# Causal attention stage: both score products of a step issued together on four row groups, its weights turned by ordinary products with the identity, and the sign of the row maximum moved to ScalarE

## The chip, the cores and the metric

One core of a Trainium2 chip. The metric is the device time of one execution in microseconds, the median of several runs: 5253.66 us before (5250.62 to 5260.75, three runs).

## The reference

Input x has 8 sequences of 512 tokens with 256 features. Four residual blocks follow each other, each on a layer norm of x: attention a (8 heads of 64), a feed-forward block f of two layers (each with windowed attention and a gated MLP), the causal attention b, and f again. All is float32. The change touches only b, which has 16 heads of 16 features:

```python
dot = jnp.einsum('bhid,bhjd->bhij', q, k)
q_norm_sq = jnp.sum(q * q, axis=-1, keepdims=True)
k_norm_sq = jnp.sum(k * k, axis=-1, keepdims=True)
vals = q_norm_sq + k_norm_sq.transpose(0, 1, 3, 2)
scores = dot * dot / (vals - 2.0 * dot + EPSILON) * SCORE_SCALE
mask = jnp.triu(jnp.ones((Lq, Lq), dtype=scores.dtype), k=1) * -1000000000.0
attn = jax.nn.softmax(scores + mask[None, None, :, :], axis=-1)
out = jnp.einsum('bhij,bhjd->bhid', attn, v)
```

So a score needs two numbers of each pair of tokens: a denominator (the squared distance plus epsilon) and the dot product for the numerator.

## The kernel before, in words

The work is a list of 48 units: 6 stages (`PLAN`: a, f, f, b, f, f) times 8 sequences. All weights of a stage are loaded once, and the activations of all sequences stay in SBUF (`resid`). Stage b is units 24 to 31.

A unit of stage b has 32 steps (`BSTEPS`). A step is two heads and one tile of 128 queries; query tile t = i % 4 sees 128 (t+1) keys, so a step's width w is 128, 256, 384 or 512 columns for each head. A step consists of parts, named in the code by `kind`:

- `bk`, `bq` (TensorE): turn 128 rows of k and q so that the features lie on partitions. A head takes 32 partitions (`BROW`), of which 16 are features and two more carry the squared norms and ones. Before the change one filling holds four heads (one per 32 rows), is done by four transposes of 128x128, and serves 8 steps; there are 4 fillings of each per unit. `bk_c`, `bq_c` (ScalarE) copy them to `k_rows`, `q_rows` (in the tile `hid`).
- `bden` (TensorE): the denominator, 18 rows deep, for the two heads; `bdot`: the dot product, 16 rows deep, for the two heads. Each is two products, on two different 32-row groups of the array; `bden` and `bdot` of a head lie on the same row group. Each takes one of the three PSUM tiles of two banks, `wide0` to `wide2`.
- `bclip` (VectorE, L1197, L1199) bounds the denominator and puts it into `b_den` (tile `w_up`); `bnum` (ScalarE, L1016) squares the numerator into `prob`.
- `bguess` (ScalarE, L1027 logarithm, L1029 exponential) makes a first reciprocal, `bclose` (GpSimd, L1414) and the first half of `bmul` (VectorE, L1207) refine it; `bmul` (VectorE, L1214, twice) multiplies it into the weights and takes each row's extreme; a last VectorE instruction of two columns (L1218) turns its sign (semaphore `neg`).
- `exp` (ScalarE, L1056, one for each head) waits for `neg`; `mask` (GpSimd, L1420) zeroes what lies above the diagonal.
- `turn_a`, `turn_b` (TensorE, L697): 2 (t+1) transposes of 128x128 into one wide tile; `pt_a` (ScalarE, L1064) and `pt_b` (VectorE, L1253) copy them out; `mix` (TensorE, L694, tile `o_ps`) multiplies them with v, two heads on two 32-column groups.
- After 8 steps `out`, `sel`, `olog`, `out_b` divide by the row sums. `proj` and `res` end the unit. The next unit's layer norm, `xt` and `bqkv` (128x512 and 128x256 products, `w_in`) run among the steps.

L694 and L697 are the lines of the helpers `mm` (matmul) and `tr` (transpose), so PE rows are told apart by their tiles. A float32 `mm` shows as two MATMUL and two LDWEIGHTS records, a `tr` as one of each.

Nothing in the engines' programs reorders work: `ordered()` writes each engine's order in advance, by a greedy pass over the parts with the costs in `cost()` and `B_COST`, the due times and the lists of what a part follows; each engine then executes its list in order, with semaphore waits in front of each part. The same pass places PSUM holders: three wide tiles and the narrow `turn_ps` (for `bk`, `bq`, `sel`). New costs thus change the order of all of stage b. Rings: `prob` has 4 buffers in stage b, `b_den`/`b_inv` 3, `pt` 2, `q_rows`/`k_rows` 2 each.

Of the kernel before, what the change touches and what calls it, by code (L numbers as in the profile page):

```python
# [8 lines left out]
ALU = mybir.AluOpType  # L9
# [62 lines left out]
for _e, _kinds in {  # L72
# [5 lines left out]
    for _k in _kinds.split():  # L78
# [3 lines left out]
B_COST = {"bclip": (0.15, 0.27), "bnum": (0.1, 0.27), "bguess": (0.25, 0.54), "bclose": (0.2, 0.6), "bmul": (0.6, 0.55),  # L82
          "exp": (0.25, 0.26), "turn_a": (0.05, 0.14), "turn_b": (0.05, 0.14), "pt_a": (0.12, 0.135),
          "pt_b": (0.12, 0.135), "mix": (0.1, 0.25), "mask": (0.8, 0.0)}


def cost(kind, u, i):
# [6 lines left out]
    if kind in ("bden", "bdot"):  # L94
        return 0.25 + 0.23 * (i % 4 + 1)
# [31 lines left out]
def parts_of(u):  # L127
# [94 lines left out]
    for k in range(steps):  # L222
# [5 lines left out]
        if st == "b":  # L228
            g = k // 8
            if k % 8 == 0:  # L230
                for kind in ("bk", "bq"):
                    put(kind, g, at - 4 / steps, final("brow", 3))
                    free = (u, 8 * (g - 1) - 1) if g >= 2 else (u - 1, 8 * (g + 3) - 1)
                    put(kind + "_c", g, at - 4 / steps, final(kind, g), ("bden", *free), ("bdot", *free),
                        ("down", u - 1, 3))
            put("bden", k, at, final("bk_c", g), final("bq_c", g))
            put("bdot", k, at, final("bk_c", g), final("bq_c", g))
            three = (u, k - 3) if k >= 3 else (u - 1, k + steps - 3)
            put("bclip", k, at, final("bden", k), ("bmul", *three), ("up_h", u - 1, 2))
# [98 lines left out]
def ordered():  # L338
# [14 lines left out]
    def ready_at(part):  # L353

        if part not in ready:
# [8 lines left out]
            for r in READERS.get(kind, ()):  # L364
                for f in parts.get((r, u, i), (0, ()))[1]:
                    if f in parts and f[0] != kind and f[0] not in READERS[kind]:
# [106 lines left out]
def build(nc, d):  # L473
    stack = ExitStack()
    with stack:
# [188 lines left out]
        def rows_free(gate, u, g):  # L664

            if g >= 2:
                gate.wait_ge(S["bden"], nth("bden", u, 8 * (g - 1) - 1))
                gate.wait_ge(S["bdot"], nth("bdot", u, 8 * (g - 1) - 1))
            elif u > 3 * SEQS:
                gate.wait_ge(S["bden"], nth("bden", u - 1, 8 * (g + 3) - 1))  # L670
                gate.wait_ge(S["bdot"], nth("bdot", u - 1, 8 * (g + 3) - 1))
# [18 lines left out]
        def tensor_program(eng):  # L690
# [9 lines left out]
            for part in ORDER["PE"]:  # L700
# [80 lines left out]
                elif kind in ("bk", "bq"):  # L781
                    pe.wait_ge(S["brow"], nth("brow", u, TILES - 1))
                    src = (k_t if kind == "bk" else q_t)[s]
                    for t in range(TILES):
                        last = tr(turn_ps[:, t * P:(t + 1) * P], src[:, i, t * P:(t + 1) * P])
# [26 lines left out]
                elif kind in ("bden", "bdot"):  # L812
                    g, t = i // 8, i % 4
                    pe.wait_ge(S["bk_c"], nth("bk_c", u, g))
                    pe.wait_ge(S["bq_c"], nth("bq_c", u, g))
                    for k in range(2):
                        r = 32 * (2 * (i // 4 % 2) + k)
                        rows = slice(r, r + BHD + (2 if kind == "bden" else 0))
# [798 lines left out]
```

## Time and profile before

| | |
|---|---|
| median of three runs | 5253.66 us |
| the profiled execution, its own time | 5240.19 us |
| its span (first to last instruction) | 5238.2 us |
| mean granted TensorE clock over the span | 0.888 |
| busy: PE, DVE, ACT, POOL | 92%, 66%, 49%, 45% |
| first and last L1218 of stage b (256 of them) | 2285.2 and 3724.0 us |

PE is TensorE's matmul record, DVE is VectorE, ACT ScalarE, POOL GpSimd. Full clock, 1.00, is 2.4 GHz, and 0.50 is 1.2 GHz. Durations of matmuls include the way through the array, so several in a row take less than their sum.

### The profile page before, as it was taken

Reading aid. Unit: us, or ns where it says so; the run is one execution under the profiler, and the core shown is the slowest. Engines: PE = TensorE matmul, PEld = TensorE weight load, DVE = VectorE, ACT = ScalarE, POOL = GpSimd, SP = SyncE. Lnnn points to the kernel's source line nnn. Section 1 sums busy time; section 2 is a strip of 40 time slices with the busy share of each in tenths; the row PEclk is TensorE's granted clock in tenths of the full one; section 3 lists DMA queues with packets and bytes.
Section 4 is the critical chain, followed back from the end, with each engine's and each line's share of the span. In section 5 each row is a group of like instructions: output and inputs, shape, how many; then the busy total and the mean of one; then the engine's idle time right before and its main releaser. Section 6 shows DMA issues by size and latency. Waiting matters only on the chain.

```text
span 5238.2 us, 66473 instructions
## 1 busy us (share of the span) xinstructions
PE 4802.2 (92%) x23008; PEld 2828.5 (54%) x23008; DVE 3440.7 (66%) x8032; ACT 2581.4 (49%) x5577; POOL 2332.9 (45%) x2331
## 2 busy tenths in 40 slices
PE   7878888999999999999999999999799999999997
PEld 4444445655555555555555555545455555555564
DVE  4554566666666666468888888878766666666653
ACT  4443444444444444356666666666544444444442
POOL 1111244544544454344555555555544544545441
PEclk9999999999999999975666666757899999999998
DMA  2000000000000000000000000000000000100000
GB/s 63 9 5 9 21 5 11 3 5 3 21 7 26 11 7 13 18 8 1 5 5 5 1 9 5 5 13 5 26 5 3 3 5 19 30 11 17 15 15 21
DMA packets 50974, 60.82 MB, mean 12 GB/s; under 512 B 11848, under 2 KB 43216, under 8 KB 50640
## 3 DMA queue, kind: packets, MB, share of 16 engines
q1 hardware_dynamic: 50640, 56.58, 3.5%
q8 instruction: 184, 3.01, 0.2%
q14 instruction: 150, 1.23, 0.1%
HBM read 35.61 MB, written 12.58 MB: 9 GB/s over the span
## 4 chain that ended last, share of the span: by engine, by line
PE 74%; DVE 15%; issue 4%; ACT 3%; POOL 3%; DMA 1%; SPq 1%; POOLq 0%; DVEq 0%; ACTq 0%
PE wide L694 51%; PE o_ps L694 10%; PE wide L697 6%; PE turn_ps L697 5%; DVE prob L1227 2%; DVE x_n L1101 1%; DVE st L1234 1%; POOL rn L1397 1%; DMA shifted<-resid 1%; DVE pt L1253 1%; DVE prob L1214 1%; SPq L1455 1%; PE turn_ps L694 1%; DVE w_down L1214 1%; ACT pt L1064 1%
## 5 line engine op out<-in xcount | busy, mean ns | idle before, releaser
L1427 POOL TENSOR_SCALAR prob<-prob,st 128x256 f32<-128x256 f32 (+1 forms) x1024 | 521.4, 529 | 972.5 <-DVE st L1240 972.2
L694 PE MATMUL wide<-w_in,x_t 128*128 128x512 f32 (+1 forms) x1792 | 850.5, 621 | 4.6 <-DVE w_up L1199 1.8
L694 PE MATMUL o_ps<-pt,v 128*64 128x256 f32 (+2 forms) x5632 | 646.9, 376 | 119.7 <-DVE pt L1253 63.9
L694 PE MATMUL wide<-x_t,w_up 128*128 128x512 f32 (+1 forms) x1536 | 698.9, 601 | 16.8 <-DVE k_t L1161 11.4
L1064 ACT ACTIVATE pt<-turn_ps 128x512 f32<-128x512 f32 x384 | 229.3, 597 | 850.4 <-PE turn_ps L697 850.4
L694 PEld LDWEIGHTS o_ps<-pt,v 128*64 128x64 f32 (+1 forms) x5632 | 391.2, 142 | 397.1 <-issue 186.1
L694 PE MATMUL wide<-hid 16*128 16x128 f32 (+7 forms) x2048 | 560.9, 662 | 41.7 <-DVE w_up L1199 27.7
L697 PE MATMUL turn_ps<-ident,prob 128*128 128x128 f32 x2816 | 466.1, 285 | 126.6 <-ACT pt L1064 122.6
L1035 ACT ACTIVATE prob<-prob,st 128x256 f32<-128x256 f32 (+1 forms) x1024 | 478.9, 472 | 189.8 <-DVE st L1227 189.7
L694 PEld LDWEIGHTS wide<-w_in,x_t 128*128 128x128 f32 x1792 | 350.2, 205 | 387.2 <-issue 379.2
L697 PEld LDWEIGHTS turn_ps<-ident,prob 128*128 128x128 f32 x2816 | 315.2, 142 | 417.9 <-issue 234.4
L694 PEld LDWEIGHTS wide<-x_t,w_up 128*128 128x128 f32 (+1 forms) x1536 | 260.7, 179 | 368.9 <-issue 347.8
L1253 DVE COPY pt<-turn_ps 128x384 f32<-128x384 f32 (+1 forms) x384 | 227.8, 593 | 299.5 <-PE turn_ps L697 299.5
L1389 POOL TENSOR_TENSOR sines<-raw,rot 128x512 f32<-128x512 f32 x256 | 386.8, 1530 | 54.8 <-ACT raw L959 54.8
L1397 POOL TENSOR_TENSOR rn<-ss,minus_half 128x16 f32<-128x16 f32 x128 | 381.1, 2977 | 51.5 <-DVE ss L1147 51.0
L1138 DVE TENSOR_TENSOR turned<-raw,rot 128x512 f32<-128x512 f32 x256 | 237.7, 969 | 229.4 <-ACT raw L959 228.5
L694 PE MATMUL wide<-k_t,q_t 64*128 64x256 f32 (+2 forms) x2560 | 364.4, 421 | 3.6 <-DVE resid L1269 2.0
L1227 DVE CUSTOM_DVE_ANT_0 prob<-wide,local_mask 128x256 f32<-128x256 f32 (+1 forms) x1024 | 332.5, 385 | 49.6 <-PE wide L694 49.6
L1430 POOL TENSOR_SCALAR prob<-prob,st 128x512 f32<-128x512 f32 x128 | 125.3, 981 | 517.7 <-DVE st L1243 517.6
L694 PEld LDWEIGHTS wide<-hid 16*128 16x128 f32 (+1 forms) x2048 | 226.2, 262 | 232.4 <-issue 157.9
L694 PE MATMUL wide<-w_out,o_t 128*128 128x256 f32 x1536 | 345.7, 384 | 5.6 <-DVE o_t L1262 2.6
L694 PE MATMUL wide<-w_down,hid 128*128 128x256 f32 x1536 | 349.3, 381 | 1.6 <-DVE hid L1325 1.6
(137 smaller groups left out, 8187.6 us busy)
## 6 DMA issues: line engine op xcount, KB each, us to landing
kept<-resid SPq DMA_DIRECT2D x16, 512.0 KB, 2.6
x_n<-kept SPq DMA_DIRECT2D x16, 512.0 KB, 3.3
shifted<-resid SPq DMA_DIRECT2D x32, 224.0 KB
w_in<-in_f_wqkv SPq DMA_DIRECT2D x4, 1536.0 KB, 6.3
w_up<-in_f_w SPq DMA_DIRECT2D x4, 1364.0 KB, 6.1
resid<-in_x SPq DMA_DIRECT2D x8, 512.0 KB, 8.2
out<-resid SPq DMA_DIRECT2D x8, 512.0 KB, 2.9
w_down<-in_f_w SPq DMA_DIRECT2D x4, 640.0 KB
```

The lines of the kernel that those rows point to most:

```text
L694: return eng.matmul(out, lhsT, rhs, start=start, stop=stop, skip_group_check=True)
L697: return eng.transpose(out, in_, ident[:, :])
L1035: last = eng.activation(pr[:, local_span(t)], pr[:, local_span(t)], ACT.Exp, bias=sm[:, t:t + 1], scale=-1.0, accum_out=sm[:, 4 + t:5 + t])
L1064: eng.activation(pt[:, 0:w], ps[:, 0:w], ACT.Copy).then_inc(S["pt_a"], 1)
L1138: last = eng.tensor_tensor(heads(out[:, side]), heads(r[:, side]), rot[:, 2 * z, i, :].unsqueeze(1).to_broadcast([P, HEADS, HD]), ALU.mult)
L1214: last = eng.tensor_tensor_reduce(pr[:, side], pr[:, side], inv[:, side], -1.0, -LOW, ALU.mult, ALU.max, sm[:, 8 + k:9 + k])
L1227: eng.tensor_tensor_reduce(pr[:, local_span(t)], ps[:, local_span(t)], local_mask[:, P if t == 0 else 0:256], -1.0, LOW, ALU.add, ALU.min, ...
L1253: eng.tensor_copy(pt[:, 512:512 + w], ps[:, 0:w]).then_inc(S["pt_b"], 1)
L1389: last = eng.tensor_tensor(halves(sines[(o - 1) % 2][:, side]), halves(r[:, side])[:, :, ::-1, :], rot[:, 2 * z + 1, i, :].rearrange("p (u ...
L1397: eng.tensor_tensor(rn[(o - 1) % 2][:, 0:16], ss[(o - 1) % 2][:, 0, :], minus_half[:, 0:16], ALU.pow).then_inc(S["rn"], 1)
L1427: last = eng.tensor_scalar(pr[:, local_span(t)], pr[:, local_span(t)], sm[:, 8 + t:9 + t], 1.0, ALU.mult, ALU.mult)
L1430: last = eng.tensor_scalar(pr[:, 0:512], pr[:, 0:512], sm[:, 4:5], 1.0, ALU.mult, ALU.mult)
```

## The change

- `bk`, `bq`: 8 fillings of each per unit, one for every 4 steps. A filling now holds two heads, each twice, in the order head 0, head 0, head 1, head 1 on the four 32-row groups. It is made by 16 ordinary products of 128 rows by 32 columns with the identity as the moving side (128 columns), each writing 32 partitions of `turn_ps`.
- `bdot` issues all four products: denominator of both heads on row groups 0 and 2, dot product of both on row groups 1 and 3. `bden` stays in the order as a part without instructions, which takes its wide tile.
- `turn_a`, `turn_b`: the transposes become ordinary products with the identity.
- The two-column change of sign goes from VectorE to ScalarE, ahead of `exp`.
- The planner's costs and lists follow.

```diff
-B_COST = {"bclip": (0.15, 0.27), "bnum": (0.1, 0.27), "bguess": (0.25, 0.54), "bclose": (0.2, 0.6), "bmul": (0.6, 0.55),
-          "exp": (0.25, 0.26), "turn_a": (0.05, 0.14), "turn_b": (0.05, 0.14), "pt_a": (0.12, 0.135),
-          "pt_b": (0.12, 0.135), "mix": (0.1, 0.25), "mask": (0.8, 0.0)}
+B_COST = {"bclip": (0.15, 0.27), "bnum": (0.1, 0.22), "bguess": (0.2, 0.47), "bclose": (0.2, 0.6), "bmul": (0.5, 0.63),
+          "exp": (0.45, 0.26), "turn_a": (0.05, 0.16), "turn_b": (0.05, 0.16), "pt_a": (0.06, 0.12),
+          "pt_b": (0.12, 0.135), "mix": (0.1, 0.28), "mask": (0.85, 0.0)}
...
-        return 0.25 + 0.23 * (i % 4 + 1)
+        return 0.1 + 0.28 * (i % 4 + 1) if kind == "bdot" else 0.0
...
-            put("bden", k, at, final("bk_c", g), final("bq_c", g))
-            put("bdot", k, at, final("bk_c", g), final("bq_c", g))
+            last = ("bdot", u, k - 1) if k else ("bdot", u - 1, steps - 1)
+            put("bden", k, at, final("bk_c", g), final("bq_c", g), last, *turned, ("down", u - 1, 3))
+            put("bdot", k, at, final("bk_c", g), final("bq_c", g), final("bden", k))
...
                     for t in range(TILES):
-                        last = tr(turn_ps[:, t * P:(t + 1) * P], src[:, i, t * P:(t + 1) * P])
+                        for r in range(4):
+                            at = t * P + BROW * (2 * (i % 2) + r // 2)
+                            last = mm(turn_ps[r * BROW:(r + 1) * BROW, t * P:(t + 1) * P], src[:, i // 2, at:at + BROW],
+                                      ident[:, :], True, True)
...
-                elif kind in ("bden", "bdot"):
-                    g, t = i // 8, i % 4
+                elif kind == "bden":
+                    continue
+                elif kind == "bdot":
+                    g, t = i // 4, i % 4
                     pe.wait_ge(S["bk_c"], nth("bk_c", u, g))
                     pe.wait_ge(S["bq_c"], nth("bq_c", u, g))
-                    for k in range(2):
-                        r = 32 * (2 * (i // 4 % 2) + k)
-                        rows = slice(r, r + BHD + (2 if kind == "bden" else 0))
-                        last = mm(ps[:, 512 * k:512 * k + P * (t + 1)], q_rows[g % 2][rows, t * P:(t + 1) * P],
-                                  k_rows[g % 2][rows, 0:P * (t + 1)], True, True)
-                    last.then_inc(S[kind], 1)
+                    for what in ("bden", "bdot"):
+                        for k in range(2):
+                            r = 2 * BROW * k + (BROW if what == "bdot" else 0)
+                            rows = slice(r, r + BHD + (2 if what == "bden" else 0))
+                            last = mm(wide[PLACE[what, u, i]][:, 512 * k:512 * k + P * (t + 1)],
+                                      q_rows[g % 2][rows, t * P:(t + 1) * P], k_rows[g % 2][rows, 0:P * (t + 1)], True, True)
+                        last.then_inc(S[what], 1)
...
-                        last = tr(ps[:, to + kb * P:to + (kb + 1) * P],
-                                  prob[SLOTS[u, i]["prob"]][:, at + kb * P:at + (kb + 1) * P])
+                        last = mm(ps[:, to + kb * P:to + (kb + 1) * P], prob[SLOTS[u, i]["prob"]][:, at + kb * P:at + (kb + 1) * P],
+                                  ident[:, :], True, True)
...
                     exp_tables()
+                    act.wait_ge(S["bmul"], nth("bmul", u, i))
+                    eng.activation(sm[:, 0:2], sm[:, 8:10], ACT.Copy, scale=-1.0).then_inc(S["neg"], 1)
                     act.wait_ge(S["neg"], nth("bmul", u, i))
...
                     last.then_inc(S["bmul"], 1)
-                    dve.wait_ge(S["bmul"], o)
-                    eng.tensor_scalar(sm[:, 0:2], sm[:, 8:10], -1.0, None, ALU.mult).then_inc(S["neg"], 1)
```

## Rows read from the trace of the kernel before

**Rows 1.** The page's slices: busy tenths in 40 slices of the span, and granted clock.
```profile
PE   7878888999999999999999999999799999999997
PEclk9999999999999999975666666757899999999998
```

**Rows 2.** Windows of stages a, f, b: length, busy us of each engine (instructions), clock.
```profile
30.00:700.00 670.00, 555.79 (x2820) 309.36 (x2820) 341.35 (x586) 292.85 (x659) 146.27 (x137) 0.97 0.02 9
852.00:2296.00 1444.00, 1359.08 (x6338) 826.34 (x6337) 903.21 (x2347) 615.87 (x1469) 690.64 (x747) 0.99 0.04 11
...
2300.00:3700.00 1400.00, 1313.21 (x6533) 739.67 (x6532) 1147.76 (x2434) 944.92 (x1715) 720.01 (x617) 0.66 0.01 5
```

**Rows 3.** Chain of waits, shares by line, 2869 to 2917 us.
```profile
by line: PE wide L694 49.2%; PE wide L697 24.5%; PE o_ps L694 17.3%; PE turn_ps L697 4.4%; PE turn_ps L694 4.2%; DVE w_up L1199 0.9%; issue 0.1%
```

**Rows 4.** Windows: a cold stretch, then one at full clock (columns of Rows 2).
```profile
2869.00:2917.00 48.00, 47.74 (x193) 26.27 (x194) 38.98 (x90) 32.88 (x59) 27.85 (x23) 0.50 0.00 1
...
2916.00:2941.00 25.00, 22.87 (x148) 12.74 (x148) 22.85 (x49) 17.55 (x33) 12.76 (x10) 0.91 0.00 1
```

**Rows 5.** Groups in stage b: count, busy us, mean ns, idle before.
```profile
L694 PE MATMUL wide<-hid 18*128 18x384 f32 (+1 forms) x1984 | 545.5, 664 | 39.3 <-DVE w_up L1199 27.7 <-DVE pt L1253 4.6 <-ACT sq L962 3.3
...
L1218 DVE TENSOR_SCALAR st<-st 128x2 f32<-128x2 f32 x248 | 134.6, 543 | 8.6
```

**Rows 6.** Windows of L697, all transposes: stages a and b (PE, PEld, clock).
```profile
30.00:700.00 670.00, 155.78 (x972) 105.17 (x972) 0.97 0.02 9
...
2300.00:3700.00 1400.00, 343.78 (x1559) 249.12 (x1558) 0.66 0.01 5
```

**Rows 7.** Windows around one rise and fall of the clock.
```profile
2654.20:2661.00 6.80, 6.63 (x15) 3.21 (x16) 5.21 (x12) 2.73 (x7) 3.34 (x4) 0.50 0.00 0
2661.00:2688.00 27.00, 26.73 (x176) 17.20 (x176) 22.59 (x50) 19.07 (x35) 14.84 (x18) 1.00 0.05 21
2691.90:2730.00 38.10, 37.68 (x171) 21.16 (x169) 29.70 (x68) 25.68 (x47) 20.61 (x18) 0.50 0.00 1
```

**Rows 8.** Timeline of PE at full clock: start, duration of the run of records.
```profile
2917.44 1.04 PE L697 MATMUL wide<-ident,w_down 128*128 128x128 f32 x8
2918.41 0.85 PE L694 MATMUL o_ps<-pt,v 128*32 128x128 f32 x12
2919.18 1.99 PE L694 MATMUL wide<-hid 18*128 18x512 f32 x8
2921.47 1.07 PE L694 MATMUL o_ps<-pt,v 128*32 128x128 f32 x16
...
2937.05 1.13 PE L694 MATMUL wide<-hid 18*128 18x512 f32 x4
```

**Rows 9.** Timeline of PE at half clock.
```profile
2952.46 1.50 PE L694 MATMUL o_ps<-pt,v 128*32 128x128 f32 x12
2953.88 2.08 PE L694 MATMUL wide<-hid 18*128 18x512 f32 x4
2955.89 1.11 PE L697 MATMUL turn_ps<-ident,q_t 128*128 128x128 f32 x4
2956.80 1.91 PE L697 MATMUL wide<-ident,w_down 128*128 128x128 f32 x8
```

**Rows 10.** Groups of ACT in stage b by shape: smallest copy, smallest exponential, a filling's copy.
```profile
L1064 ACT ACTIVATE pt<-wide 128x128 f32<-128x128 f32 x62 | 16.7, 269 | 0.0
L1056 ACT ACTIVATE prob<-prob,st 128x128 f32<-128x128 f32 x124 | 42.4, 391 | 2.4 <-DVE st L1218 2.4
L1008 ACT ACTIVATE hid<-turn_ps 128x512 f32<-128x512 f32 x30 | 17.6, 587 | 0.0
```

**Rows 11.** Line L1218: durations ns min/median/max, first and last start.
```profile
L1218 DVE TENSOR_SCALAR st<-st x256: 168/169/2321, 2285.2 to 3724.0; 128x2 f32<-128x2 f32 x128
```

**Rows 12.** Timeline: GpSimd and VectorE side by side.
```profile
2916.42 1.81 POOL L1414 TENSOR_TENSOR w_up<-w_up,x_t 128x768 f32<-128x768 f32 x1 [0.65 <-ACT x_t L1029]
2916.45 1.81 DVE L1218 TENSOR_SCALAR st<-st 128x2 f32<-128x2 f32 x1
```

More of the change, by code:

```diff
@@ L228, in parts_of @@
         if st == "b":
-            g = k // 8
-            if k % 8 == 0:
+            g = k // 4
+            if k % 4 == 0:
                 for kind in ("bk", "bq"):
                     put(kind, g, at - 4 / steps, final("brow", 3))
-                    free = (u, 8 * (g - 1) - 1) if g >= 2 else (u - 1, 8 * (g + 3) - 1)
-                    put(kind + "_c", g, at - 4 / steps, final(kind, g), ("bden", *free), ("bdot", *free),
-                        ("down", u - 1, 3))
-            put("bden", k, at, final("bk_c", g), final("bq_c", g))
-            put("bdot", k, at, final("bk_c", g), final("bq_c", g))
+                    free = (u, 4 * (g - 1) - 1) if g >= 2 else (u - 1, 4 * (g + 7) - 1)
+                    put(kind + "_c", g, at - 4 / steps, final(kind, g), ("bdot", *free), ("down", u - 1, 3))
+            last = ("bdot", u, k - 1) if k else ("bdot", u - 1, steps - 1)
+            put("bden", k, at, final("bk_c", g), final("bq_c", g), last, *turned, ("down", u - 1, 3))
+            put("bdot", k, at, final("bk_c", g), final("bq_c", g), final("bden", k))
             three = (u, k - 3) if k >= 3 else (u - 1, k + steps - 3)
-            put("bclip", k, at, final("bden", k), ("bmul", *three), ("up_h", u - 1, 2))
+            put("bclip", k, at, final("bdot", k), ("bmul", *three), ("up_h", u - 1, 2))
             put("bnum", k, at, final("bdot", k), *turned, ("down", u - 1, 3))
@@ L365, in ready_at @@
                 for f in parts.get((r, u, i), (0, ()))[1]:
-                    if f in parts and f[0] != kind and f[0] not in READERS[kind]:
+                    if f in parts and f[0] != kind and f[0] not in READERS[kind] and f != ("bdot", u, i):
                         if f not in end:
@@ L666, in rows_free @@
             if g >= 2:
-                gate.wait_ge(S["bden"], nth("bden", u, 8 * (g - 1) - 1))
-                gate.wait_ge(S["bdot"], nth("bdot", u, 8 * (g - 1) - 1))
+                gate.wait_ge(S["bdot"], nth("bdot", u, 4 * (g - 1) - 1))
             elif u > 3 * SEQS:
-                gate.wait_ge(S["bden"], nth("bden", u - 1, 8 * (g + 3) - 1))
-                gate.wait_ge(S["bdot"], nth("bdot", u - 1, 8 * (g + 3) - 1))
+                gate.wait_ge(S["bdot"], nth("bdot", u - 1, 4 * (g + 7) - 1))
             else:
```

## The prediction

> **What bounds the kernel now.** I read the page's slices first [rows 1]: TensorE (PE) is above 90% busy nearly everywhere, and its granted clock is near 1 except in twelve slices in the middle, which are stage b. The windows put numbers on it [rows 2]: stage f has PE at 94% and clock 0.99; stage b has PE at 94% too (1313 of 1400 us) but clock 0.66, with DVE at 82%, ACT at 67% and POOL at 51%. The 256 steps of b span about 1440 us [rows 11]. The chain of waits over a cold stretch is 99% PE [rows 3], and there PE is busy 47.7 of 48.0 us while DVE has 39.0 [rows 4]. At nearly full clock the picture turns: in 2916 to 2941 DVE is busy 22.85 of 25 us, PE 22.87 and with idle gaps. So b is bound by PE at half clock, and DVE stands right behind it.
>
> Why is the clock low? PE is no less busy than in f. What differs is the kind of work: 545 us of b's PE time are score products 16 or 18 rows deep on two 32-row groups [rows 5], 344 us are transposes [rows 6]; together two thirds. The clock rose after a stretch of few, long records that fill the array (15 matmul records in 6.8 us) and fell back among steps (171 in 38 us), with PE 97 to 99% busy on both sides [rows 7]. Transposes alone don't do it: stage a has 156 us of them in 670 us and a clock of 0.97, but its other products are 64 to 128 rows deep. Thus shallow products and transposes together leave the clock low, by these rows.
>
> **The change part by part**, PE first, at full clock (2.4 GHz); at half clock (1.2 GHz) it takes about double.
>
> Scores. A score product of 512 columns and its partner take 1.13 us, denominator and numerator together 1.99 us [rows 8]. Per 128 columns a single float32 product costs about 0.22 us: mix goes from 0.85 us (12 records, three rounds of two side by side) to 1.07 us (16 records, four rounds). With four products side by side a step of tile t saves 0.22 (t+1) us, on average 0.22 x 2.5 = 0.545, x256 = 140 us. That four run together is not in the trace; two do. Bound from the other side: two at a time, saving nothing. I take four, since they use disjoint row groups as the two do now.
>
> Turns. A transpose costs (1.04 - 0.17)/8 = 0.109 us, an ordinary product two records of that, 0.218. There are 2 (t+1) per step, 5 on average: 5 x 0.109 = 0.545, x256 = 140 us more. Scores and turns cancel, at either clock.
>
> Fillings. There are 64 of bk and bq now, 1.11 us each at half clock [rows 9], 0.60 at full (4 x 0.109 + 0.17). After, 128, each 16 products on four column groups: four rounds of two records, eight slots of 0.109 plus 0.2 = 1.07 us (1.9 at half clock). That adds 128 x 1.07 - 64 x 0.60 = 98 us at full clock, 172 at half. If only two column groups work together, as mix shows, it is 128 x 0.87 = 111 us more; if products with the half-sized weight side cost less, at most the 98 goes.
>
> So at an unchanged clock PE has about 100 to 170 us more to do. Everything hangs on the clock. Work of 1313 us at a mean of 0.66 is 867 us at full clock, some 890 with the fixed 0.2 us of each run of products; plus 98 is about 990, at a clock of 0.97 (stage a's) 1015 us per 1400 us of today's stage. And the clock should come: of a step's PE time after the change the turns (1.3 us of about 3.7) and the fillings (0.5) fill the array with ordinary products, the scores hold four row groups in place of two, and mix and bqkv stay. Full-array work per stage rises by 140 x 2 + 128 x 0.87 = 390 us within some 1200. That is denser than stage a, which holds 0.97 with PE only 83% busy.
>
> On this point the Trainium skill has a sentence in each direction. "TensorE: Matmul & The Clock Gate", Part 4, says a transpose-mode product doesn't count as busy for the clock; by it the turns alone would lift the clock, and the trace agrees as far as b's cold stretches are rich in them. "Perfetto Trace Analysis", section Transposes, says to use transposes, not standard matmuls, for a transpose; by it the change of the turns is a loss. No row here shows a float32 product with the identity that is not a transpose; by the rows of mix it costs what is written above under Turns, and the second rival carries it.
>
> VectorE. L1218 goes: 134.6 us per 1400 [rows 5]. Its median is 169 ns, its mean 543 [rows 11]: the rest is waiting beside a GpSimd instruction, seen at 2916.45, where both last 1.81 us [rows 12]. Part of that wait may reappear at L1214, next to which POOL runs more densely: I add 30 (bounds 0 and 90). DVE: 1148 - 135 + 30 = 1043.
>
> ScalarE. It gets 256 copies of two columns. The trace has no such shape; the smallest copy of 128 columns takes 0.269 us, the smallest exponential 0.391 [rows 10]. Taking 0.25 near the former: 248 x 0.25 = 62 (40 to 97); queued behind it are this step's two exponentials, which waited for L1218 anyway. Plus 64 more copies of fillings at 0.587, 37 us. ACT: 945 + 62 + 36 = 1043. GpSimd keeps 720.
>
> So three engines have 1015 to 1043 us each in place of one with 1313. What share can the busiest reach? DVE reached 0.91 in the stretch at high clock [rows 4], where PE had slack; with three equals and orders fixed in advance I take 0.89: 1043/0.89 = 1172, times 1440/1400 = 1206 us. Saved: 1440 - 1206 = 234. The profiled execution took 5240.2 (2 outside the span), so 5006; the median of the three stands 13.5 above it, so about **5020**. At 0.94 (PE in f) it is 1141 and 4955; at 0.83 (PE in a) 1292 and 5106.
>
> What is late next: DVE, mostly at L1214 and L1207, with ACT on its heels; the edge of PSUM too, since both scores now want two of three wide tiles at once.
>
> **Rivals.**
>
> 1. Clock rises, but the queues block each other. bdot starts only when two wide tiles are free, the turns hold the third, and the next step's scores wait for L1197/L1199 on a DVE that is full. Holding times per step are about 2.0 (denominator), 1.8, 2.0 and 1.0 for the unit's other products, 6.8 us over three tiles or 2.3 us a step against 4.7 available: for it speaks only that PE's queue is in order; against it the slack. Price: half a microsecond a step on the 1206, 128 us: 5020 + 128 = 5150.
>
> 2. The other side: the clock stays. It decides if the granted clock of b remains below about 0.8. PE then carries scores and turns that cancel, plus fillings, 98 to 172 us, about 150, at 94 to 99% busy; nothing else matters. 5254 + 150 = 5400. For it: PE was 97% busy in the cold and that didn't help, so density must really change; against it, stage a.
>
> 3. Scores run two at a time. PE gets 140 us more, 1155 per 1400, and binds again: at 0.94, 1229, times 1.03 = 1264 us, 5078. For it: no four at once in the trace.
>
> **How the numbers follow.** Forecast 0.62; rival 1, 0.16; rival 2, 0.10; rival 3, 0.12. The likeliest time is 5020. Its own range, from the shares 0.94 and 0.83 and the bounds of ACT and DVE, is 4940 to 5110; to leave out only about 2 in 10 I stretch it over the third rival and the first: 4930 to 5185. A measurement of this kernel can tell about 0.2% (10 us) from no change. Faster: 0.87, the forecast and rivals 1 and 3, less a little for fillings that cost more than I think; slower 0.10, rival 2; same 0.03.
>
> **What the profile after would show.** Right: b's granted clock above 0.93; score records of 16 and 18 rows starting together, and a run of 512 columns for both lasting 1.1 to 1.3 us; eight turns as 16 records in about 1.9 us; fillings of 32 records in about 1.1 us; L1218 gone, a two-column ACT copy of 0.2 to 0.3 us; DVE near 88% busy in b; its chain mixed of DVE, PE and ACT; stages a and f unchanged to 10 us. Wrong: clock in b below 0.8 and a chain all of PE (rival 2); at full clock, PE idle on L1199 or L1016 with DVE under 80% (rival 1); score runs of 1.9 us at full clock (rival 3).

## The result, and the profile after

The changed kernel takes 5186.4 us (median of four runs, 5166.7 to 5202.4) against 5252.1 us: a ratio of 0.9872 with a 95% interval of 0.9835 to 0.9910. It is faster by 66 us, where 5020 us was forecast with a range of 4930 to 5185. The time lies 1.4 us outside the range, and the gain is little more than a quarter of the forecast 232 us. The profiled execution is the fastest of the four, 5166.7 us.

The page's slices after, beside [rows 1]: tenths of busy time, and the granted clock.
```profile
PE   7878888999999999998888888878899999999997
...
PEclk9999999999999999998888898889899999999998
```
In the middle PE fell from 9 to 8 tenths (7 in one slice) while the clock rose from 5 to 8 tenths to 8 and 9. The other slices are unchanged or nearly so. The window of stage b after, columns as in [rows 2]: length, then busy us (instructions) of PE, PEld, DVE, ACT and POOL, clock.
```profile
2290.00:3668.00 1378.00, 1154.70 (x11777) 817.28 (x11768) 1091.02 (x2273) 1059.22 (x2092) 759.72 (x645) 0.87 0.02 6
```
The steps of b span 1372 us (first to last start of the instruction shown below), where they spanned 1439 [rows 11]: 67 of the 74 us by which the profiled execution is shorter (span 5164.3 us for 5238.2). No engine is at 90%: PE has 84%, DVE 79%, ACT 77%, POOL 55%. The chain of waits of stage b, by line, first before (2300 to 3700 us), then after (2300 to 3600 us):
```profile
by line: PE wide L694 39.0%; PE wide L697 16.3%; PE o_ps L694 13.1%; issue 4.7%; DVE prob L1214 3.4%; PE turn_ps L694 3.3%; DVE w_down L1214 2.9%; PE turn_ps L697 2.7%; DVE x_t L1207 2.2%; DVE x_n L1207 2.1%; DVE hid L1207 2.0%; DVE w_up L1
```
```profile
by line: PE wide L692 33.6%; issue 9.5%; PE o_ps L692 7.2%; PE turn_ps L692 6.1%; DVE prob L1220 5.2%; POOL w_up L1418 4.6%; DVE w_down L1220 4.1%; DVE hid L1213 2.5%; DVE x_t L1213 2.3%; ACT prob L1062 2.2%; DVE x_n L1213 1.7%; DVE shifted
```
The lines of PE had 74% of the chain before and have 47% after; PE is still its largest part, with the other engines now sharing the rest. "Issue" is time in which an engine waited for nothing that the profile shows. `mm` is now L692 and `tr` L695, so a turn by a product stands under L692.

The single operations, from PE's timeline (start, us; beside [rows 8]):
```profile
2862.07 2.05 PE L692 MATMUL wide<-ident,w_down 128*128 128x128 f32 x16 [0.36 <-DVE raw L1183]
...
2867.08 1.07 PE L692 MATMUL o_ps<-pt,v 128*32 128x128 f32 x16
2868.08 1.14 PE L692 MATMUL wide<-hid 18*128 18x512 f32 x8
2869.15 1.08 PE L692 MATMUL turn_ps<-ident,k_t 128*32 128x128 f32 x32
```
Denominators and dot products of 512 columns together take 1.14 us, where they took 1.99; a filling of 16 products takes 1.08; eight turns take 2.05, where the transposes took 1.04 and I had reckoned with 1.9. The same timeline, a little earlier, shows what the mean hides:
```profile
2852.59 1.65 PE L692 MATMUL turn_ps<-ident,q_t 128*32 128x128 f32 x32 [2.95 <-DVE o_t L1266]
...
2875.08 0.71 PE L692 MATMUL wide<-hid 18*128 18x256 f32 x8 [1.96 <-ACT prob L1020]
```
PE stood for 2.95 us before the filling, the clock fell to half at 2852.9 while the filling ran, and it took 1.65 us in place of 1.08. The pause of 1.96 us is followed by the next fall, at 2876.8.
```profile
2852.00:2860.00 8.00, 6.67 (x60) 4.96 (x61) 4.86 (x11) 3.15 (x7) 1.03 (x1) 0.57 0.00 0
```
The line is the window of those 8 us, columns as before: PE's clock is 0.57. Over the stage PE idles 223 us (1378 - 1155). The trace's clock falls to half 56 times within the steps of b, for 341 us in all and never for more than 10.3 us at a time; before, it fell 32 times, for 980 us in all and up to 181 us at a time.

ScalarE's new instruction, as the view of its line shows it: durations in ns (min/median/max), first and last start.
```profile
L1058 ACT ACTIVATE st<-st x256: 186/196/224, 2296.6 to 3668.4; 128x2 f32<-128x2 f32 x128
```

### The profile page after: what moved, and what is told of

Same layout as the page of the kernel before. It is cut to its first block, busy times and chain, and to the rows that moved or that the text cites. A ratio compares the mean times of both kernels' runs of the same rounds, so it can differ in the third digit from the quotient of the medians.

```text
span 5164.3 us, 76918 instructions
## 1 busy us (share of the span) xinstructions
PE 4604.0 (89%) x28128; PEld 2885.9 (56%) x28128; DVE 3328.0 (64%) x7776; ACT 2660.6 (52%) x5897; POOL 2332.1 (45%) x2331
## 4 chain that ended last, share of the span: by engine, by line
PE 67%; DVE 16%; ACT 6%; issue 5%; POOL 4%; DMA 1%; SPq 1%; DVEq 0%; POOLq 0%; ACTq 0%
PE wide L692 50%; PE o_ps L692 9%; PE turn_ps L695 5%; PE wide L695 2%; PE turn_ps L692 2%; DVE prob L1231 2%; DVE prob L1220 1%; DVE x_n L1107 1%; POOL w_up L1418 1%; DMA shifted<-resid 1%; DVE st L1238 1%; DVE w_down L1220 1%; DVE pt L1257 1%; ACT pt L1070 1%; SPq L1459 1%
## 5 line engine op out<-in xcount | busy, mean ns | idle before, releaser
L692 PE MATMUL wide<-w_in,x_t 128*128 128x512 f32 (+1 forms) x1792 | 828.9, 608 | 2.3 <-ACT x_t L956 1.3
L692 PE MATMUL o_ps<-pt,v 128*64 128x256 f32 (+2 forms) x5632 | 598.8, 353 | 186.8 <-DVE pt L1257 82.5
L692 PE MATMUL wide<-x_t,w_up 128*128 128x512 f32 (+1 forms) x1536 | 697.8, 601 | 15.7 <-DVE k_t L1167 11.4
L692 PEld LDWEIGHTS o_ps<-pt,v 128*64 128x64 f32 (+1 forms) x5632 | 369.2, 133 | 430.5 <-issue 168.3
L695 PE MATMUL turn_ps<-ident,prob 128*128 128x128 f32 x2816 | 467.6, 286 | 125.8 <-ACT pt L1070 121.3
L695 PEld LDWEIGHTS turn_ps<-ident,prob 128*128 128x128 f32 x2816 | 316.3, 142 | 420.6 <-issue 237.8
L692 PEld LDWEIGHTS wide<-w_in,x_t 128*128 128x128 f32 x1792 | 339.8, 200 | 361.9 <-issue 357.3
L692 PEld LDWEIGHTS wide<-x_t,w_up 128*128 128x128 f32 (+1 forms) x1536 | 260.5, 179 | 367.6 <-issue 347.7
L692 PE MATMUL wide<-k_t,q_t 64*128 64x256 f32 (+2 forms) x2560 | 362.2, 419 | 2.3 <-DVE k_t L1167 2.2
L692 PE MATMUL wide<-w_down,hid 128*128 128x256 f32 x1536 | 349.1, 381 | 1.6 <-DVE hid L1329 1.6
L692 PE MATMUL wide<-w_out,o_t 128*128 128x256 f32 x1536 | 339.9, 379 | 2.0 <-ACT o_t L1080 1.9
L692 PEld LDWEIGHTS wide<-w_out,o_t 128*128 128x128 f32 x1536 | 291.0, 190 | 56.3 <-issue 18.4
L692 PEld LDWEIGHTS wide<-w_down,hid 128*128 128x128 f32 x1536 | 284.8, 190 | 39.6 <-DVE hid L1329 2.5
```

The source lines that it names most:

```text
L692: return eng.matmul(out, lhsT, rhs, start=start, stop=stop, skip_group_check=True)
L695: return eng.transpose(out, in_, ident[:, :])
```

## The experiments

In every edit below, orders of all engines stay as in the kernel named, unless it says that they change. Ratios are against the kernel before, run beside it on the same chip, with 95% intervals.

**First round: each part undone or done alone.** The theory then was that the products with the identity lift the clock and that this is the gain.

e1, the changed kernel with transposes for the turns:
```diff
-                        last = mm(ps[...], prob[...][...], ident[:, :], True, True)
+                        last = tr(ps[...], prob[...][...])
```


> The changed kernel with its turns of stage b as transposes again; every engine's order as in the changed kernel. Theory (the products with the identity are what lifted the clock): the granted clock of stage b falls from 0.87 to about 0.70 and the time rises to 5230 to 5300 us although TensorE has 140 us less to do at full clock. Rival (four row groups and the column-tiled fillings lifted the clock): the clock stays at 0.85 or more and the time falls to 5100 to 5150 us.

Measured: 5132.6 us, ratio 0.9769 (0.9751 to 0.9786), 54 us faster than the change, and the theory fell. The window of its stage b, columns as above:
```profile
2292.00:3654.00 1362.00, 1097.64 (x10538) 687.18 (x10528) 1076.24 (x2276) 1061.44 (x2096) 756.13 (x645) 0.79 0.02 6
```
The clock did fall, from 0.87 to 0.79, but not to where it had been, and PE is busy 57 us less all the same. The products lift the clock and cost more than they lift. The 140 us of added work at full clock came out as 57 us of busy time. Not all of that is time of the stage: PE's idle is 41 us longer in e1 (264 for 223), and from first to last instruction of the sign the steps span 1353 us for 1372. The 54 us are between medians; how the profiled executions divide their 31 us is told behind the third round.

e4, the reverse: the kernel before with only the turns as products (the edit of e1 the other way round).

> The kernel before with only its turns of stage b as ordinary products with the identity; orders, layout and costs of before kept. Theory (the products lift the clock and that is the whole gain): the clock of stage b rises from 0.66 to 0.85 or more, and although TensorE gets 140 us more at full clock the time falls to 5130 to 5210 us. Rival (the other parts lifted the clock; by itself the product is only dearer than a transpose): the clock stays below 0.75 and the time rises by 100 to 280 us to 5350 to 5530.

Measured: 5253.5 us, ratio 1.0012 (0.9998 to 1.0027): no change. The window of its stage b:
```profile
2289.00:3742.00 1453.00, 1314.33 (x7975) 871.88 (x7975) 1185.18 (x2512) 981.32 (x1767) 747.72 (x635) 0.81 0.01 5
```
The same window of the kernel before:
```profile
2281.00:3724.00 1443.00, 1348.31 (x6714) 759.21 (x6716) 1184.23 (x2514) 975.14 (x1767) 741.15 (x635) 0.66 0.01 5
```
The clock rose from 0.66 to 0.81 by this edit alone, PE is busy 34 us less, and nothing came of it. So clock and time are different things here. Neither the theory (a gain) nor its rival (a loss) was right: gain of clock and cost of work cancel in the kernel before, and e1 shows a loss in the changed one.

e2, both dot products on the row groups of the denominators:
```diff
-                            r = 2 * BROW * k + (BROW if what == "bdot" else 0)
+                            r = 2 * BROW * k
```


> The changed kernel with both dot products on the row groups of the denominators, so that only two of the four score products can run together; orders kept. Theory (TensorE's length still counts in stage b): a run for 512 columns lasts 2.0 us in place of 1.14, 140 us more work at full clock, the time rises by 60 to 140 us to 5250 to 5330. Rival (stalls of the in-order queue set the time and absorb it): less than 30 us more.

Measured: 5246.5 us, ratio 0.9987 (0.9977 to 0.9996), so four at once are worth 60 us in the changed kernel, of 140 us of work at full clock, at the lower edge of the 60 to 140 expected.

e3, the sign back on VectorE:
```diff
-                    act.wait_ge(S["bmul"], nth("bmul", u, i))
-                    eng.activation(sm[:, 0:2], sm[:, 8:10], ACT.Copy, scale=-1.0).then_inc(S["neg"], 1)
...
+                    dve.wait_ge(S["bmul"], o)
+                    eng.tensor_scalar(sm[:, 0:2], sm[:, 8:10], -1.0, None, ALU.mult).then_inc(S["neg"], 1)
```


> The changed kernel with the change of sign back on VectorE; orders kept. Theory (VectorE's port waits count): the instruction takes about 0.5 us again on the mean, the time rises by 30 to 80 us to 5215 to 5265. Rival (neither engine is the bound, each at under 0.8 of the stage): within 15 us of 5186.

Measured: 5256.0 us, ratio 1.0007 (0.9994 to 1.0020): 70 us more, all of the change's gain. The instruction is the old one again, with a median of 169 ns and a longest of 2374, in the view of its line:
```profile
L1222 DVE TENSOR_SCALAR st<-st x256: 168/169/2374, 2304.5 to 3762.1; 128x2 f32<-128x2 f32 x128
```
ScalarE stood 180 us until this instruction, ahead of the exponentials; in the changed kernel it stands 103 us ahead of its own copy. The window of stage b:
```profile
2300.00:3763.00 1463.00, 1179.26 (x11743) 838.93 (x11744) 1203.32 (x2530) 1023.44 (x1837) 759.91 (x645) 0.86 0.02 5
```
The stage is 85 us longer than the change's, PE is busy only 25 us of them and idle the other 60: here the sign costs through waits, not through PE's clock.

**Second round: does the smallest edit do it alone, and is the plan to blame?**

e5, the kernel before with only the sign on ScalarE (the edit of e3 reversed).

> The kernel before with only the change of sign moved to ScalarE; orders, layout, costs and transposes of before kept. Theory (several engines share the path, and this one edit shortens VectorE by 0.47 us a step wherever it is put): the time falls by 40 to 80 us to 5170 to 5210. Rival (before, TensorE at half clock is the only bound, 93% busy, so VectorE's relief is hidden and pays only once TensorE is relieved): within 20 us of 5252.

Measured: 5206.8 us, ratio 0.9903 (0.9873 to 0.9934), 51 us less by the ratio, although PE still was the busiest engine by far, as the window of its stage b shows:
```profile
2294.00:3691.00 1397.00, 1283.93 (x6712) 728.36 (x6710) 1086.54 (x2257) 1017.93 (x2022) 737.30 (x635) 0.70 0.01 5
```
PE is 92% busy here, at a clock of 0.70. That relief on an engine at 82% shortens a stage in which PE has 94% speaks against the reading that PE's work alone is the bound. It doesn't show through what it came: the clock rose from 0.66, and PE's busy time fell by 64 us at the same work (1348 x 0.66 = 890, 1284 x 0.70 = 899), which is more than the stage's 46.

e6, e1 with each filling by four transposes (it leaves out the doubling of the heads, so the scores mix heads):
```diff
-                        for r in range(4):
-                            at = t * P + BROW * (2 * (i % 2) + r // 2)
-                            last = mm(turn_ps[r * BROW:(r + 1) * BROW, t * P:(t + 1) * P], src[:, i // 2, at:at + BROW],
-                                      ident[:, :], True, True)
+                        last = tr(turn_ps[:, t * P:(t + 1) * P], src[:, i // 2, t * P:(t + 1) * P])
```


> As e1 (changed kernel, turns as transposes), with each filling of k and q made by four transposes of 128x128 in place of 16 products. This leaves out the doubling of the heads, so denominators and dot products of a step are of different heads; amounts and orders are the same. It prices the fillings. Theory (they cost 0.5 us each at full clock, 128 of them, and lift the clock little): the time falls by 30 to 60 us against e1's 5133, clock 0.74 to 0.79. Rival (the fillings' products are what lifts e1's clock to 0.79 from 0.66): the clock falls to 0.70 or less and the time rises above 5150.

Measured: 5133.9 us, ratio 0.9760 (0.9728 to 0.9792), the same as e1, where 30 to 60 us less was expected. The steps of b tell it otherwise: they span 1332 us, 20 us less than e1's 1353, with PE's work at full clock 65 us less (1078 x 0.74 = 798 for 1092 x 0.79 = 863). The rest of the program took 14 us longer in the profiled execution than in e1's, and hides it. One execution of each tells no more than that the fillings may cost some 20 us. The edit gives back only what 16 products cost more than four transposes, 60 of the 98 us that I had priced (128 x (1.07 - 0.60)); that there are twice as many fillings stays in.

e10, e1 with measured costs in the planner (orders change):
```diff
-B_COST = {"bclip": (0.15, 0.27), "bnum": (0.1, 0.22), "bguess": (0.2, 0.47), "bclose": (0.2, 0.6), "bmul": (0.5, 0.63),
-          "exp": (0.45, 0.26), "turn_a": (0.05, 0.16), "turn_b": (0.05, 0.16), "pt_a": (0.06, 0.12),
+B_COST = {"bclip": (0.2, 0.29), "bnum": (0.1, 0.22), "bguess": (0.2, 0.47), "bclose": (0.2, 0.6), "bmul": (0.6, 0.8),
+          "exp": (0.5, 0.3), "turn_a": (0.1, 0.13), "turn_b": (0.05, 0.13), "pt_a": (0.13, 0.12),
...
-            "bk": 0.6, "bq": 0.6, "proj": 1.9, "xt2": 1.2, "up_g": 3.6, "up_h": 3.6, "down": 2.8,
+            "bk": 1.05, "bq": 1.05, "proj": 1.9, "xt2": 1.2, "up_g": 3.6, "up_h": 3.6, "down": 2.8,
```


> As e1, with the planner's costs of stage b set to what the trace measured (fillings 1.05 in place of 0.6, VectorE's multiplication 0.6 + 0.8 per 128 columns in place of 0.5 + 0.63, exponentials, bounding and copies a little more, transposes 0.13 per block), so all orders of stage b change. Theory (the idle of 16 to 20% on TensorE comes from orders planned with costs that are too small): TensorE idles less, the time falls by 20 to 60 us against e1 to 5075 to 5115. Rival (the waits come from the dependencies and the three PSUM tiles, not from the costs): within 20 us of 5133.

e11, e1 with `sel` in a wide tile (orders change):
```diff
-NARROW = ("bk", "bq", "turn_a", "turn_b", "sel")
+NARROW = ("bk", "bq", "turn_a", "turn_b")
...
-                    mm(turn_ps[:, :], sum_rows[:, :], o_raw, True, True).then_inc(S["sel"], 1)
+                    mm(ps[:, 0:512], sum_rows[:, :], o_raw, True, True).then_inc(S["sel"], 1)
...
-                    eng.activation(b_weight, turn_ps[:, :], ACT.Ln).then_inc(S["olog"], 1)
+                    eng.activation(b_weight, wide[PLACE["sel", u, i]][:, 0:512], ACT.Ln).then_inc(S["olog"], 1)
...
```


> As e1, with the product of the row sums (sel) in one of the three wide PSUM tiles in place of turn_ps, so that the fillings no longer wait for the division of the group before. Theory (the waits of the fillings for o_t, some 37 us of TensorE's idle in the changed kernel, end the path): 15 to 40 us less than e1's 5133. Rival (the wide tiles are scarcer than the narrow one): 10 to 60 us more.

Measured: e10 5141.9 us (0.9779, 0.9753 to 0.9806) and e11 5151.5 us (0.9793, 0.9759 to 0.9827). Better costs don't help, and neither does freeing the narrow tile; both theories missed. In the profiled executions the steps of b span 1346 and 1351 us, where e1's span 1353.

**Third round: what holds all engines at 80%?**

e14, e1 with GpSimd's product in `bclose` cut to 16 columns (most of the refinement is left out):
```diff
-                    eng.tensor_tensor(den, den, inv, ALU.mult).then_inc(S["bclose"], 1)
+                    eng.tensor_tensor(den[:, 0:16], den[:, 0:16], inv[:, 0:16], ALU.mult).then_inc(S["bclose"], 1)
```


> As e1, with GpSimd's product in bclose cut to 16 columns of a step's 256 to 1024, which leaves most of the refinement of the reciprocal out. GpSimd loses about 370 of its 756 us in stage b, and VectorE the waits beside it. Theory (the engines walk in lockstep, the path goes through all of them, GpSimd's latency too): the time falls by 80 to 160 us against e1's 5133 although GpSimd is only 56% busy. Rival (GpSimd is off the path): less than 40 us.

Measured: 5008.8 us, ratio 0.9534 (0.9514 to 0.9554), 124 us below e1. The window of its stage b:
```profile
2290.00:3502.00 1212.00, 1025.82 (x10537) 645.33 (x10526) 971.59 (x2275) 1052.36 (x2093) 412.18 (x645) 0.84 0.02 6
```
With this product out of the way the stage is 1212 us long, and the busiest engine, now ScalarE, reaches 87%. That this is nearly the 1206 us that I had forecast is in part luck: DVE has 972 us here and PE 1026, less than the changed kernel's 1091 and 1155. DVE lost 105 us of busy time (55 of them in the multiplications into the weights, L1220, and 25 in L1213) though its work is unchanged, so that much was waiting inside its instructions beside GpSimd; PE lost 72, and times the clock its work is the same (1098 x 0.79 = 867, 1026 x 0.84 = 862). The chain of waits of the changed kernel had given the product only 4.6% (POOL w_up L1418), 60 us of 1300: cutting it was worth twice that.

e15, e1 with four buffers between `bclip` and `bmul`, in all units but the last (orders change; the waits for a free buffer change with it and aren't shown):
```diff
-        b_inv = [..., b_hid[:, 2048:3072]]
+        b_den.append(sines[0][:, :])
+        b_inv = [..., b_hid[:, 2048:3072], sines[1][:, :]]
```


> As e1, with four buffers for the denominators and reciprocals in place of three (the fourth in the tiles of the sines, which stage b does not use; the last unit keeps three); the orders change with it. Theory (the ring between bclip and bmul, 8 us long and three steps deep, keeps the engines at 0.79): the time falls by 20 to 60 us. Rival (PSUM and PE's order set the pace): within 20 us of 5133.

e18, e1 with `HOP = 0.35` for 0.2 (orders change):

> As e1, with the planner's time for a hop between engines at 0.35 in place of 0.2, which changes the orders of all stages. Theory (orders matter by chance only, a per cent either way): within 40 us of 5133. Rival (the plan is too tight for the real hops): 20 to 60 us less.

e20, e1 with denominators and dot products as two parts again (orders change, and so do the parts' costs and the waits for them):
```diff
-            put("bden", k, at, final("bk_c", g), final("bq_c", g), last, *turned, ("down", u - 1, 3))
-            put("bdot", k, at, final("bk_c", g), final("bq_c", g), final("bden", k))
+            put("bden", k, at, final("bk_c", g), final("bq_c", g))
+            put("bdot", k, at, final("bk_c", g), final("bq_c", g))
...
-                    for what in ("bden", "bdot"):
+                    for what in (kind,):
...
```


> As e1, with denominators and dot products of a step as two parts again, each with its own tile and wait, on the new row groups, so that the denominator can start when one wide tile is free; orders change. Theory (the demand for two of three wide tiles at once stalls TensorE, my first rival): the time falls by 20 to 60 us, TensorE's idle ahead of the scores shrinks. Rival (what four at once gains is lost when the two parts come apart): 20 to 80 us more.

Measured: e15 5150.9 us (0.9807, 0.9793 to 0.9822), e18 5179.4 (0.9864, 0.9842 to 0.9887), e20 5181.9 (0.9871, 0.9852 to 0.9890). A fourth buffer doesn't help. e18 is 47 us worse, more than the 40 expected, and e20 costs 49 us against e1.

Here the whole times mislead. The steps of b, from the first to the last instruction of the sign, and all that lies before and behind them, in the profiled execution of each kernel (us; e21 and e22 are of the fourth round):

| kernel | span | steps of b | before and behind |
|---|---|---|---|
| before | 5238.2 | 1438.8 | 3799.4 |
| the change | 5164.3 | 1371.8 | 3792.5 |
| e1 | 5133.4 | 1352.7 | 3780.7 |
| e6 | 5126.9 | 1332.4 | 3794.5 |
| e10 | 5142.5 | 1345.5 | 3797.0 |
| e11 | 5150.8 | 1350.7 | 3800.1 |
| e14 | 4991.8 | 1204.1 | 3787.7 |
| e15 | 5153.4 | 1351.3 | 3802.1 |
| e18 | 5171.8 | 1342.7 | 3829.1 |
| e20 | 5172.0 | 1366.3 | 3805.7 |
| e21 | 5067.6 | 1284.5 | 3783.1 |
| e22 | 5181.5 | 1389.3 | 3792.2 |

What lies behind the steps, with the same work, first in the change and then in e1:
```profile
3668.40:5164.30 1495.90, 1389.88 (x6481) 848.19 (x6480) 895.63 (x2351) 625.82 (x1516) 672.49 (x732) 0.97 0.05 15
```
```profile
3652.70:5133.40 1480.70, 1373.80 (x6466) 839.47 (x6464) 896.11 (x2351) 625.88 (x1516) 673.83 (x732) 0.98 0.05 15
```
So of the 31 us between these two executions 19 are the steps' and 15 lie behind them (ahead of them 3 us go the other way). Behind them PE was busy 16 us less at a clock of 0.98 for 0.97. Of all the runs only e1 and e21 have 0.98 there. Why they do is open. One execution of each is profiled, and those of the changed kernel differ by 36 us among themselves, so the steps are known to some 20 us.

With that, e10, e11, e15 and e18 are not worse than e1 in the stage that they were made for: 1343 to 1351 us for 1353. e18's 47 us lie outside the steps, since `HOP` changes the orders of all stages. Four other plans of b thus move its steps by 10 us at most, where 166 are to be explained (1372 for the forecast 1206). That is evidence against a large effect of the costs, the narrow tile, the ring or the hop, and no evidence on smaller ones.

e20 doesn't settle what it was made for. PE's timeline in it:
```profile
2864.55 0.70 PE L694 MATMUL wide<-hid 18*128 18x256 f32 x4
2869.30 1.22 PE L694 MATMUL wide<-hid 16*128 16x256 f32 x4 [4.05 <-DVE w_up L1205]
```
Denominators and dot products come apart by over 4 us, and within the steps PE is busy 1191 us for e1's 1092. The edit takes away the demand for two tiles at once and the four at once together. That the steps lose only 14 us by it leaves room for a gain from the first. The waits of PE in the changed kernel, 2300 to 3600 us (us in total, times, longest), say more:
```profile
PE o_ps L692 <- ACT pt L1070: 53.9, 33, 3.0
...
PE wide L692 <- ACT prob L1020: 14.8, 14, 2.0
...
PE wide L692 <- DVE w_up L1205: 10.8, 9, 4.5
```
PE idles 208 us there. The readers of the score tiles, L1020 and L1205, end 26 of them; the largest wait is that of `mix` for the copied turns.

**Fourth round: GpSimd's latency, or the waits beside it?**

e21, e1, in six of the eight units: GpSimd multiplies data of the sines in place of the denominators, and VectorE goes on without its result, so that the refinement of the reciprocal is left out there:
```diff
-                    dve.wait_ge(S["bclose"], o)
-                    eng.scalar_tensor_tensor(out=inv, in0=den, scalar=2.0, in1=inv, op0=ALU.subtract, op1=ALU.mult
+                    dve.wait_ge(S["bguess"], o)
+                    eng.scalar_tensor_tensor(out=inv, in0=inv, scalar=-1.0, in1=den, op0=ALU.mult, op1=ALU.min
...
-                    eng.tensor_tensor(den, den, inv, ALU.mult).then_inc(S["bclose"], 1)
+                        eng.tensor_tensor(sines[0][:, 0:n2], sines[1][:, 0:n2], sines[1][:, 0:n2], ALU.mult
+                                          ).then_inc(S["bclose"], 1)
```


> As e1, but in six of the eight units of stage b GpSimd's product of bclose works on other data of the same size (the tiles of the sines), and VectorE goes on without it with an instruction of the same shape; the refinement of the reciprocal is left out there. GpSimd's work and its reading beside VectorE stay. Theory (GpSimd's latency in the chain of a step is what held the engines apart): the time falls by 60 to 110 us against e1's 5133. Rival (it is VectorE's waiting beside GpSimd's reads): less than 25 us.

Measured: 5071.9 us, ratio 0.9659 (0.9639 to 0.9679), 61 us below e1, the lower edge of the theory's 60 to 110. GpSimd keeps its work (685 us of 1295, 53%; e1 has 756 of 1362, 56%), and DVE's own busy time is nearly e1's (1062 for 1076 us). The window of its stage b:
```profile
2295.00:3590.00 1295.00, 1041.76 (x10561) 654.71 (x10561) 1062.24 (x2276) 1057.71 (x2096) 684.82 (x646) 0.83 0.02 6
```
The groups of GpSimd's product, first in e1 and then in e21 (count, busy us, mean ns, idle before):
```profile
L1418 POOL TENSOR_TENSOR w_up<-w_up,x_t 128x256 f32<-128x256 f32 (+1 forms) x86 | 144.4, 1680 | 113.6 <-ACT x_t L1033 113.5
```
```profile
L1432 POOL TENSOR_TENSOR sines<-sines 128x256 f32<-128x256 f32 x192 | 253.1, 1318 | 261.2 <-ACT x_t L1033 89.6 <-ACT x_n L1033 86.7 <-ACT hid L1033 84.3
```
The product off the chain takes 1.32 us in place of 1.68, so e21 takes away a little of GpSimd's work too, and isn't a clean measure of the latency alone. Six of eight units gave 61 us, so all eight would give about 80 (estimate: 61 x 8/6), some two thirds of e14's 124; by the steps of b it is 68 us, about 90 for all eight, of 149. So GpSimd's latency in the chain of a step seems the larger part of e14's gain; the rest would go with the shorter busy time of DVE there.

e22, e1 with `bclose` and the first multiplication by halves:
```diff
+                    for k in range(2):
+                        eng.tensor_tensor(den[:, k * half:(k + 1) * half], den[:, k * half:(k + 1) * half],
+                                          inv[:, k * half:(k + 1) * half], ALU.mult).then_inc(S["bclose"], 1)
...
```


> As e1, with bclose and VectorE's first multiplication each in two instructions, one for each head, so that VectorE starts when the first half is there. Theory of latency: the chain of a step is 0.7 us shorter, the extra instructions cost VectorE and GpSimd 0.1 to 0.2 us each; the time falls by 10 to 40 us against 5133. Rival (waits beside GpSimd): two instructions of GpSimd give VectorE more to wait for, 0 to 30 us more.

Measured: 5171.6 us, ratio 0.9850 (0.9827 to 0.9873), 39 us more than e1. The theory of latency had forecast 10 to 40 us less, its rival up to 30 more; both missed. GpSimd and DVE each issue twice as many instructions there as before, and within the steps DVE is busy 45 us longer (1118 for 1073) and GpSimd 58 (813 for 755). That seems to outweigh the earlier start, so this run doesn't support the latency, nor does it refute it.

e25, e1 with the sign on VectorE (the edit of e3 on e1): scores, fillings and costs alone.

> As e1, with the change of sign on VectorE again: of the change only the four score products together, the fillings and the planner's costs are left. If the parts add up, the sign is worth 46 us (e5) to 70 us (e3), so 5133 + 46 to 70 = 5180 to 5205 us. If the sign's gain needs a relieved TensorE, more than 5215.

Measured: 5220.5 us, ratio 0.9935 (0.9913 to 0.9957): the parts don't add up, as the second theory had it. The table of the parts, each against the kernel before (ratio minus one, times 5252):

| parts | us |
|---|---|
| turns by products alone (e4) | +6, within noise |
| sign alone (e5) | -51 |
| four scores, fillings, costs (e25) | -34 |
| both of these (e1) | -121 |
| and turns by products (the change) | -67 |

Sign and scores together bring 36 us more than the sum of both, with an uncertainty of some 20 us from the three intervals; the products take 54 away, with about the same uncertainty.

## Why the prediction was wrong

- **The works of the engines** were right. For the whole stage I had DVE at 1074 us (1043 x 1.03), measured 1091; ACT 1074, measured 1059; PE 1013 at full clock (1044 x 0.97), measured 1155 x 0.87 = 1005. Scores (1.14 us) and fillings (1.08) had the durations of the sum to a few hundredths of a microsecond, a run of eight turns took 2.05 for 1.9, and four scores did run together, so the third rival fell. A slip in the sum, 990 us at a clock of 0.97, which is 1021 and not 1015, changes nothing in the forecast, since DVE and ACT at 1043 carry it. ScalarE's copy takes 0.196 us, where I had taken 0.25.
- **The step that failed** is the share of the stage that the busiest engine reaches: "with three equals and orders fixed in advance I take 0.89". Measured: 0.84 for PE, which spends 111 us more than forecast because of the clock, and 0.79 for DVE. I took the 0.91 of one high-clock stretch of 25 us [rows 4] and the 0.94 of a stage with a single loaded engine [rows 2] for a stage with three. e14 shows that 0.87 is within reach once GpSimd's 1.68 us are out of each step's chain: its steps are 149 us shorter than e1's, and e1's were 147 us above the forecast (1353 for 1206). e21 makes it likely that some two thirds of e14's gain go back to GpSimd's latency, though it is 55% busy; the rest is VectorE's waiting beside it. GpSimd I had carried as "keeps 720", an amount, and asked nothing of its place in the chain. Even in e14 DVE has only 0.80, so part of the distance stays unexplained.
- **The clock** rose, but to 0.87 and not above 0.93, while PE's idle went from 87 of 1400 us [rows 2] to 223 of 1378. At 2852 an idle of 2.95 us is followed by a stretch at half clock. I had taken stage a, with 83% busy and 0.97, as proof that idle doesn't matter; its idle is spread otherwise. Counted in the traces, PE pauses for more than 2 us twice in the 670 us of stage a, and 27 times in the 1372 us of the steps after.
- **Turns by products**: I had it that they cancel the scores, and that they pay by the clock. e1 refutes the second half: 54 us faster without them (19 in the steps of b, in the profiled executions), at a clock of 0.79. Four scores and fillings had lifted the clock from 0.66 to 0.76 already (e25). On the two rules weighed: replacing the transposes alone did lift the clock from 0.66 to 0.81 (e4). By "TensorE: Matmul & The Clock Gate" of the Trainium skill, Part 4, that was to be expected, and the run agrees. By "Perfetto Trace Analysis" of the Trainium skill, section Transposes, they should have stayed transposes, and e1 agrees: that advice gave the time.
- **The sign** I had treated as 135 us off DVE and 62 on ACT, hidden in the shares. It is the best single edit: 51 us alone, and taking it back costs the whole gain (e3). The old instruction waited up to 2.3 us beside GpSimd, between the row maximum and the exponential. In the trace of the kernel before, 80 of its 256 executions last longer than 0.3 us, and each of these ends within 0.2 us of the end of a GpSimd instruction beside it. That its length counts because it stands in the chain of a step, and not because VectorE is that much fuller, fits ScalarE's 180 us of waiting for it in e3, but no run tells the two apart.
- **Rival 1** (queues block each other at a risen clock, 5150) was the nearest in time, and DVE under 80% (0.79) was one of its signs. The other, PE idle on the readers of the score tiles, came small: 26 of 208 us. So its mechanism, two of three wide tiles at once, isn't what did most of it; e20, made to try it, lost the four at once as well and proves neither. Rival 2 (clock stays) fell with the clock.

What stays open: how much of the remaining distance is the plan's. Four other plans moved the steps of b by 10 us at most, but no search for a better one was made. That the half-clock stretches are caused by the idle ahead of them was seen in the timeline, not tried by an edit of its own.

The best version that leaves nothing out is e1: the change without its turns by products, 5132.6 us, 2.3% below the kernel before and 1.0% below the change.

## What to carry to other kernels

When the bound engine is relieved, the new time isn't the next engine's busy time over a share borrowed from a stretch with one loaded engine: follow one step through all engines and count the latencies, an engine at half load included. A higher granted clock is no gain by itself; ask what work bought it. A two-column instruction that waits beside GpSimd can be worth more than a hundred microseconds of matmul work: 70 us here (e3), where 140 us of score products at full clock were worth 60 (e2). And compare the stage that an edit touches, not the whole time alone: e18 lost 47 us, none of them in the stage at hand.

## What the runs showed of the hardware

- Four float32 products on four 32-row groups run as fast as two: 1.14 us for 512 columns, where two took 1.13 [rows 8]. Sixteen products on four column groups take 1.08 us, 32 records at 34 ns each. Turns by products took 1.16 us for 8 records and 2.05 for 16 at full clock, so about 0.22 us per 128x128.
- A VectorE instruction of 128x2, median 169 ns, lasted up to 2.3 us, and all 80 of its long executions in the kernel before end with a GpSimd instruction. The same two columns on ScalarE took 186 to 224 ns.
- The granted clock of stage b: 0.66 before, 0.70 with the sign moved (e5), 0.76 with four scores at once (e25), 0.79 with both (e1), 0.81 with only the turns as products (e4), 0.87 with all, 0.90 with all and the scores two at a time (e2). The order of these is not the order of the times.
